# Batch 0's first steps reordered, one table set for exponential and logarithm, raw weights without a ring, later low parts beside main 0

## What is computed

```
x = x + ssm(layernorm(x))        # projection, depthwise conv + silu, selective scan over 512 rows, output product
x = x + ffn(layernorm(x))        # 8 experts: silu(x w_gate) * (x w_up), w_down, weighted by two softmaxes
x = x + attention(layernorm(x))  # 16 heads of 8, chunks of 10 rows, 25 rows to the left
x = x + ffn(layernorm(x))        # the same experts again
```

## Time and profile before

| | |
|---|---|
| median of 3 runs | 1492.82 us (1489.45 to 1494.48) |
| the profiled execution | 1493.85 us, span 1492.1 us |
| mean granted TensorE clock | 0.994 |
| PE busy | 1427.2 us, 96% |
| DVE, ACT, POOL busy | 950.3, 773.0, 504.3 us |
| first expert matmul (main 0) | 55.24 us |
| first expert matmul of main 1 | 143.2 us |
| table loads | 1.28 us each |

### The profile page before, as it was taken

The page is one execution under the profiler, slowest core; times in us unless marked ns, Lnnn a source line. Parts: engine busy times, 40 slices in busy tenths (PEclk is TensorE's granted clock), DMA queues, the critical chain, the costliest instruction groups (busy, mean ns, idle before and its releaser), DMA issues.

```text
span 1492.1 us, 31350 instructions
## 1 busy us (share of the span) xinstructions
PE 1427.2 (96%) x12756; PEld 1236.2 (83%) x12756; DVE 950.3 (64%) x2125; ACT 773.0 (52%) x1037; POOL 504.3 (34%) x446
## 2 busy tenths in 40 slices
PE   5798999999999999999999999999999999999998
PEld 3587878888788888888888888888888888888887
DVE  5655686665856667567675785658755565566543
ACT  6364738653466545645456574555644444355321
POOL 4351553433423443135410671136503320331000
PEclk9999999999999999999999999999999999999999
DMA  5120341004210420124002500062004200510000
GB/s 170 52 58 15 102 123 31 16 15 121 40 38 23 135 40 1 45 99 83 9 2 81 137 8 9 2 164 61 1 2 121 40 2 1 138 24 2 1 7 8
DMA packets 82876, 75.50 MB, mean 51 GB/s; under 512 B 5532, under 2 KB 60860, under 8 KB 82732
## 3 DMA queue, kind: packets, MB, share of 16 engines
q1 hardware_dynamic: 82732, 73.50, 18.8%
HBM read 60.65 MB, written 12.83 MB: 49 GB/s over the span
## 4 chain that ended last, share of the span: by engine, by line
PE 77%; DVE 10%; ACT 5%; issue 5%; POOL 4%; DMA 1%; DVEq 0%; SPq 0%; POOLq 0%; ACTq 0%
PE pd L1003 25%; PE pg L275 7%; PE pu L275 7%; PE pg L277 6%; PE pu L276 6%; PE pg L276 6%; PE pu L277 6%; PE att_ps L680 3%; DVE h L1096 2%; PE att_ps L702 2%; POOL arena L631 1%; PE att_ps L707 1%; DVE ffn_rows L298 1%; POOL arena L633 1%; DVE x L1084 1%
## 5 line engine op out<-in xcount | busy, mean ns | idle before, releaser
L1058 ACT ACTIVATE h<-pg 128x512 f32<-128x512 f32 x512 | 303.5, 597 | 658.3 <-PE pg L277 655.2
L1003 PEld LDWEIGHTS pd<-w_down,h 128*128 128x128 f32 x4096 | 512.2, 192 | 31.8 <-issue 2.7
L1003 PE MATMUL pd<-w_down,h 128*128 128x128 f32 x4096 | 525.0, 276 | 0.8 <-DVE x L1084 0.8
L1096 DVE TENSOR_TENSOR h<-h,pu 128x512 f32<-128x512 f32 x512 | 345.5, 679 | 215.4 <-PE pu L277 213.9
L275 PE MATMUL pg<-ffn_x_hi,w_gate_hi 128*128 128x512 f32 x512 | 244.5, 477 | 1.5 <-DVE ffn_x_lo L358 1.5
L275 PE MATMUL pu<-ffn_x_hi,w_up_hi 128*128 128x512 f32 x512 | 205.3, 401 | 13.4 <-DVE h L1096 13.2
L276 PE MATMUL pu<-ffn_x_lo,w_up_hi 128*128 128x512 f32 x512 | 203.3, 397 | 0.0
L276 PE MATMUL pg<-ffn_x_lo,w_gate_hi 128*128 128x512 f32 x512 | 203.3, 397 | 0.0
L277 PE MATMUL pg<-ffn_x_hi,w_gate_lo 128*128 128x512 f32 x512 | 203.0, 397 | 0.0
L277 PE MATMUL pu<-ffn_x_hi,w_up_lo 128*128 128x512 f32 x512 | 202.9, 396 | 0.0
L905 POOL TENSOR_TENSOR att_arena<-att_arena 128x512 f32<-128x512 f32 (+1 forms) x72 | 72.8, 1011 | 352.6 <-DVE att_arena L777 352.3
(11 more groups left out here) (192 smaller groups left out, 1540.2 us busy)
## 6 DMA issues: line engine op xcount, KB each, us to landing
arena<-bc_spread SPq DMA_DIRECT2D x56, 256.0 KB, 4.8
att_arena<-v_rows SPq DMA_DIRECT2D x64, 144.0 KB, 4.0
qk_rows<-qk_parts SPq DMA_DIRECT2D x32, 256.0 KB, 2.3
q<-qk_rows SPq DMA_DIRECT2D x32, 256.0 KB, 3.6
k<-qk_rows SPq DMA_DIRECT2D x32, 256.0 KB, 4.5
att_arena<-v_rows SPq DMA_DIRECT2D x64, 128.0 KB, 3.4
arena<-in_x SPq DMA_DIRECT2D x8, 256.0 KB, 2.9
x<-in_x SPq DMA_DIRECT2D x8, 256.0 KB, 3.4
```

The costliest lines, as they stand in the source:

```text
L1003: last = nc.tensor.matmul(pd[:, t * P:(t + 1) * P], h_b[:, d % NH, t * P:(t + 1) * P], wd[:, d % NCH, :], start=d % CPE == 0 and t == 0, s ...
L1058: nc.scalar.activation(h_b[:, c % NH, :], pg[c % 2][:, :], ACT.Silu).then_inc(gate_done, 1)
L1096: nc.vector.tensor_tensor(h, h, pu[d % 2][:, :], ALU.mult).then_inc(h_done, 1)
```

## The change

- The transposes of batch 0 come before the two products of small weights on PE, which are a job of their own now (slots -32.5 and -30.5); DVE's work on the second moves behind the convolution, and `w_small` counts one more step.
- PE makes the B/C product of batch 0 before the dt product.
- The SiLU of z moves behind the masked copy, for all batches, with a semaphore of its own (`silu_z`). The lower 64 rows of `zb` are set to zero once by POOL, and the z product reads all 128 rows.
- Behind tanh ACT loads the table set `natural_log_exp_and_others` explicitly; the copy of the tanh rows then comes before the exponential.
- The raw blocks have 16 places: the eight of `h_b` and eight in the part of the attention's buffer that is not in use yet. SP waits for none of them. Blocks alternate gate and up, so block j belongs to expert j // 2.
- ACT makes the high parts one slot earlier (from -33, ahead of the copy at -32.5).
- POOL makes the low parts 0 to 7 as before and the low parts 8 to 15 in slots -2 to 1, two in each. PE waits at every fourth chunk of main 0 for the two low parts of that expert; ACT waits at chunk 0 for eight.
- PE waits for `w_down` at the first down product.

The core of the diff:

```diff
+        w_raw = [h_b[:, i, :] for i in range(NH)] + [att_ar[:, N_S + i * L:N_S + (i + 1) * L] for i in range(2 * E - NH)]
...
                 if i == 0:
                     pe.wait_ge(w_small, 1)
+
+                    pe.wait_ge(xs_done, 1)
+                    for v in range(2):
+                        last = nc.tensor.matmul(pd[0:2 * DSTATE, :], wbc[v][:, :], xs, start=v == 0, stop=v == 1)
+                    last.then_inc(bc_raw, 1)
...
+                if i == 0:
+                    pe.wait_ge(pads_set, 9)
+                pe.wait_ge(silu_z, i + 1)
+
                 for t in range(TT):
-                    nc.tensor.matmul(ps[:, t * P:(t + 1) * P], zb[0:INNER, t * P:(t + 1) * P],
-                                     pk("w_out_z")[0:INNER, :], start=t == 0, stop=False)
+                    nc.tensor.matmul(ps[:, t * P:(t + 1) * P], zb[:, t * P:(t + 1) * P], pk("w_out_z"), start=t == 0, stop=False)
...
-                nc.scalar.activation(zb[0:INNER, :], cv[INNER:P, :], ACT.Silu).then_inc(silu_x, 1)
-                act.wait_ge(silu_x, 3 * i + 2)
+                act.wait_ge(silu_x, 2 * i + 2)
                 nc.scalar.activation(xsm, xb2, ACT.Copy, scale=pk("lo_ssm")).then_inc(xs_m, 1)
+                nc.scalar.activation(zb[0:INNER, :], cv[INNER:P, :], ACT.Silu).then_inc(silu_z, 1)
...
-                    rates(link)
+                    act.preload_act_table_set("natural_log_exp_and_others")
                     act.wait_ge(bc_set, 1)
                     nc.scalar.copy(bc_part[0], bc_t[:, :]).then_inc(bc_hi, 1)
+                    rates(link)
                     link.wait()
                     nc.scalar.activation(delta, delta, ACT.Ln, bias=1.0).then_inc(dt_soft, 1)
                     act.wait_ge(delta_done, 1)
+                    act.wait_ge(w_small, 2)
...
         def w_part(j, v):
-            return (wg, wu)[j // E][v][:, CPE * (j % E):CPE * (j % E + 1), :].rearrange("p a b -> p (a b)")
+
+            return (wg, wu)[j % 2][v][:, CPE * (j // 2):CPE * (j // 2 + 1), :].rearrange("p a b -> p (a b)")
...
                     if c == 0:
-                        pe.wait_ge(w_lo, 2 * E)
-                        pe.wait_ge(wd_loaded, 16 * E)
                         pe.wait_ge(pads_set, 8)
+                    if c < NCH and c % CPE == 0:
+                        pe.wait_ge(w_lo, 2 * (c // CPE + 1))
...
+                def small_weights(pe, link, k):
+
+                    yield T_SSM[0]["ln"] + 0.5
+                    pe.wait_ge(raw_packed, 16)
+                    nc.tensor.matmul(pg[0][:, 0:P], pk("w_dtx")[0:DTRANK, :], pk("w_dt")[0:DTRANK, :],
+                                     start=True, stop=True).then_inc(wdt_full, 1)
+                    yield T_SSM[0]["win"] + 0.5
...
-                        if j >= NH:
-                            sp.wait_ge(w_lo, j - NH + 1)
-                        sp.dma_start(h_b[:, j % NH, :], (wg_d, wu_d)[j // E][j % E]).then_inc(w_loaded[j % NH], 16)
+                        sp.dma_start(w_raw[j], (wg_d, wu_d)[j % 2][j // 2]).then_inc(w_loaded[j], 16)
...
                     if c < 0:
-                        if 0 <= c + SETUP - 8 < 2 * E:
-                            split_w(c + SETUP - 8)
+                        if 0 <= c + SETUP - 7 < 2 * E:
+                            split_w(c + SETUP - 7)
                         return
...
                 def chunk(c):
-                    if c < 0:
-                        j = c + SETUP - 8
-                        if 0 <= j < 2 * E:
+                    if c < 0 and 0 <= c + SETUP - 8 < NH:
+                        split_w(c + SETUP - 8)
+
+                    if -2 <= c < 2:
+                        for j in range(NH + 2 * (c + 2), NH + 2 * (c + 3)):
                             split_w(j)
-                        return
                     yield
...
+                pool.wait_ge(pads_set, 8)
+                nc.gpsimd.memset(zb[INNER:P, :], 0.0).then_inc(pads_set, 1)
+                pool.wait_ge(pads_set, 9)
```

More of the change, by code:

```diff
@@ L190, in build @@
         res_loaded = [sem(f"res_loaded{i}") for i in range(NXB)]
-        w_loaded, wd_loaded = [sem(f"w_loaded{i}") for i in range(NH)], sem("wd_loaded")
+        w_loaded, wd_loaded = [sem(f"w_loaded{i}") for i in range(2 * E)], sem("wd_loaded")
         w_hi, w_lo, w_small, w_prep, wdt_full = sem("w_hi"), sem("w_lo"), sem("w_small"), sem("w_prep"), sem("wdt_full")
@@ L203, in build @@
         bc_out = sem("bc_out")
-        silu_x, xs_m, xs_done = sem("silu_x"), sem("xs_m"), sem("xs_done")
+        silu_x, silu_z, xs_m, xs_done = sem("silu_x"), sem("silu_z"), sem("xs_m"), sem("xs_done")
         dt_soft, delta_done = sem("dt_soft"), sem("delta_done")
@@ L403, in pe @@
                 if i == 0:
-                    for v in range(2):
-                        last = nc.tensor.matmul(pd[0:2 * DSTATE, :], wbc[v][:, :], xs, start=v == 0, stop=v == 1)
-                    last.then_inc(bc_raw, 1)
                     yield at["k"][0] - 0.5
@@ L877, in pool @@
                 if j == 0:
-                    pool.wait_ge(w_small, 2)
+                    pool.wait_ge(w_small, 3)
                 heads = pk("head").unsqueeze(1).unsqueeze(3).broadcast_to([P, 4, 4, QW])
@@ L998, in chunk @@
                         pe.wait_ge(h_done, d + 1)
+                        if d == 0:
+                            pe.wait_ge(wd_loaded, 16 * E)
                         if d % CPE == 0 and d:
@@ L1008, in _ @@
                 pe.wait_ge(packed, 16)
[L1009 to L1015, removed]
+                def small_weights(pe, link, k):
[4 more added lines that the diff above has]
+                    yield T_SSM[0]["win"] + 0.5
+                    nc.tensor.matmul(pg[1][:, 0:P], pk("b_v").broadcast_to([P, P]), pk("w_o"),
+                                     start=True, stop=True).then_inc(bias_full, 1)
+                interleave([(small_weights, 0)] + [(Ssm.pe, i) for i in range(B)] + [(Att.pe, j) for j in range(B)] + [(Head.pe, m) for m in range(NM)], pe, None, chunk)
             @block.sync
@@ L1042, in split_w @@
                 def split_w(j):
-                    act.wait_ge(w_loaded[j % NH], 16 * (j // NH + 1))
-                    nc.scalar.copy(w_part(j, 0), h_b[:, j % NH, :]).then_inc(w_hi, 1)
+                    act.wait_ge(w_loaded[j], 16)
+                    nc.scalar.copy(w_part(j, 0), w_raw[j]).then_inc(w_hi, 1)
                 def chunk(c):
                     if c < 0:
-                        if 0 <= c + SETUP - 8 < 2 * E:
-                            split_w(c + SETUP - 8)
+                        if 0 <= c + SETUP - 7 < 2 * E:
+                            split_w(c + SETUP - 7)
                         return
@@ L1053, in chunk @@
                         if c == 0:
-                            act.wait_ge(w_lo, 2 * E)
-                            act.wait_ge(w_small, 2)
+                            act.wait_ge(w_lo, NH)
+                            act.wait_ge(w_small, 3)
                         if c >= NH:
@@ L1119, in small_weights @@
                     link(nc.vector.tensor_copy(u_b[:, 0, 0:P], pg[0][:, 0:P]))
-                    both([w[:, :] for w in wdt], u_b[:, 0, 0:P])
+                    link(nc.vector.tensor_copy(wdt[0][:, :], u_b[:, 0, 0:P]))
+                    nc.vector.tensor_tensor(wdt[1][:, :], u_b[:, 0, 0:P], wdt[0][:, :].bitcast(F32),
+                                            ALU.subtract).then_inc(w_small, 1)
+                    yield T_SSM[0]["win"] + 1.5
                     dve.wait_ge(bias_full, 1)
@@ L1125, in small_weights @@
                     nc.vector.tensor_scalar(neg_a[:, :], neg_a[:, :], -1.0, -1e-4, ALU.mult, ALU.add).then_inc(w_small, 1)
-                    dve.wait_ge(w_small, 1)
                     yield T_SSM[0]["y"]
@@ L1141, in split_w @@
                     pool.wait_ge(w_hi, j + 1)
-                    nc.gpsimd.tensor_tensor(w_part(j, 1), h_b[:, j % NH, :], w_part(j, 0).bitcast(F32),
+                    nc.gpsimd.tensor_tensor(w_part(j, 1), w_raw[j], w_part(j, 0).bitcast(F32),
                                             ALU.subtract).then_inc(w_lo, 1)
                 def chunk(c):
-                    if c < 0:
-                        j = c + SETUP - 8
-                        if 0 <= j < 2 * E:
+                    if c < 0 and 0 <= c + SETUP - 8 < NH:
+                        split_w(c + SETUP - 8)
+                    if -2 <= c < 2:
+                        for j in range(NH + 2 * (c + 2), NH + 2 * (c + 3)):
                             split_w(j)
-                        return
                     yield
```

## The result

| | before | changed |
|---|---|---|
| median | 1492.31 us (14 runs, 1488.67 to 1494.86) | 1485.82 us (14 runs, 1483.20 to 1489.76) |
| ratio to before | | 0.9954, 95% interval 0.9944 to 0.9965 |
| profiled execution | 1493.85 us, span 1492.1 | 1483.2 us, span 1481.4 |
| residual add of batch 0 | 48.62 us | 38.17 us |
| first expert matmul | 55.24 us | 48.62 us |

The change makes the kernel 6.5 us faster, 0.46%. The measured time lies inside the forecast's range of 1483.8 to 1494.8, but the forecast was 2.65 us faster, and it gave "within 0.3%" the largest chance. Both collisions of DVE's rows with POOL's low parts happened as forecast; what was too low is the rest of the gain.

A forecast was written before the change was run, and what follows sets the result against it. The prediction took a latency chain of batch 0 as the bound before 55.24 us, then PE. Its terms, -4.35 + 1.2 + 1.0 - 0.3 - 0.2 = -2.65 us from the median 1492.82, gave 1490.0 us, range 1483.8 to 1494.8.

The forecast's parts named there:

- within 0.3%: The outcome that the changed kernel differs from the one before by at most about 4.5 us; chance 0.55.
- Both collisions: DVE's rows in main 0's and batch 1's norms wait for POOL's low parts: 3.85 us more, then PE stands 1.2.
- Front: Start of batch 0: ACT's copy of the transposed rows starts at 9.6 to 9.65, gain 0.3 us, bounds 0 and 1.2.
- SiLU, order of the small products, tanh: Batch 0's chain: moving z's SiLU saves 0.6 us, B/C before dt 0.87; tanh comes about 1.6 us earlier.
- Tables: Between tanh and decays: one table set saves two loads of 1.28 us each; decays start at 23.5, 3.7 earlier.
- DVE without POOL: From batch 0's decays to residual add: with POOL silent, scans and products save 4.5 us; residual add at 40.4.
- a later rise of the clock: In main 0: PE's short stop puts off the rise to the high clock, costing 1.0 us, bounds 0 and 3.4.
- Rival C: Around main 0: held rows and PE's stops make the clock's rise fail, so the kernel is slower, 1497.5 us; chance 0.08.
- The z product: In the output product: reading 128 rows in place of 64, with as many matmuls and columns, costs nothing.
- the likeliest case: Both collisions happen and one table set serves between tanh and decays; 1487 to 1493 us, chance 0.50.
- rival A: Norms of main 0 and batch 1: no collision of DVE's rows with POOL's low parts; 1484.2 us, chance 0.25.

The follow-up runs named there:

- e5_z128_alone: The kernel before with one part alone: POOL zeroes the lower 64 rows of zb and PE's z product reads all 128; 1492.72 us, ratio 0.9994.
- e8_before_guard: The kernel before plus one wait: POOL waits for the four row blocks after its power in state space and expert norms; 1482.28 us, ratio 0.9927.
- e7_old_order: The changed kernel with z's SiLU again ahead of the masked copy and batch 0's dt product ahead of its B/C product; 1487.71 us, ratio 0.9973.
- e3_no_set: The changed kernel without the explicit load of the table set, so three loads stand between tanh and decays; 1488.15 us, ratio 0.9972.
- e2_low_early: The changed kernel with all 16 low parts made by POOL before main 0, directly behind the high parts; 1488.84 us, ratio 0.9973.
- e1_low_late: The changed kernel with low parts 8 to 15 made in slots 2 to 5, after a wait for batch 1's normalised rows; 1481.35 us, ratio 0.9929.
- e4_z64: The changed kernel with the z product read from 64 rows again, the zero fill kept; 1491.70 us, ratio 0.9990.

## Why the prediction was right and wrong, point by point

**Front.** Forecast: copy at 9.6, bound by a weight landing 6.3 us after its issue. Measured 8.62: the load landed after 5.3, and the cast and the transposes both ended at 8.6. Over all eleven profiles, with this or the old front, the copy starts anywhere from 8.4 to 9.95; the profile of before, from which I took the landing, was the latest. In e5_z128_alone and e8_before_guard, with the old front, it started at 9.09 and 8.66 and the first expert matmul came at 54.4 and 54.0, not 55.24. So about 1 us of the 6.6 us between the two profiles is the landings of two executions. One profile gave me one draw of a duration, and I used it as the value. Between the two profiles the term is 1.33, just outside its bounds of 0 and 1.2. Over the profiles the mean start is 8.75 with the new front (eight) and 9.23 with the old one (three), 0.5 apart, near the 0.3 of the forecast.

**SiLU, order of the small products, tanh.** Forecast 4.26 us from SiLU to tanh, measured 4.28; e7_old_order shows the 1.3 us of the two edits.

**Tables.** Forecast 4.32 from tanh to decays, measured 4.29; e3_no_set gives 2.2 for the two loads. The draining time that "ScalarE: Activation LUTs" of the Trainium skill adds to each load, in "What ACT_TABLE_LOAD costs", did not show: in e3_no_set the next operation starts within 0.02 us, three times.

**DVE without POOL.** Forecast 16.9 from decays to residual add, measured 15.8. The scans are 1.22 and the products 0.69 as forecast:

```profile
28.85 0.69 DVE L546 SCALAR_TENSOR_TENSOR arena<-x,arena 128x512 f32<-128x512 f32 x1
29.45 1.22 DVE L556 TENSOR_TENSOR_SCAN arena<-arena 128x512 f32<-128x512 f32 x1
```

I had left out one clip and one cast that were also slow beside POOL in the kernel before:

```profile
33.81 0.85 DVE L531 TENSOR_SCALAR x<-x 128x512 f32<-128x512 f32 x1
...
46.37 0.50 DVE L1104 CAST w_q_hi<-staged 128x128 fp32r<-128x128 f32 x1
```

In the changed kernel they take 0.42 and 0.22: 0.7 us. The last two blocks of the output product ran at the high clock (1.06 and 1.16 us for eight records, against 2.09), which kept PE out of the way; this is the 0.3 that the forecast had booked under the clock. e2_low_early puts the whole of it at 5.7 instead of 4.5.

**The collisions.** Forecast 5.0 us for the rows, measured 4.95; the last row of batch 1 forecast 1.2 us too late for PE, measured 1.5 (chunk 2 starts 7.88 us after chunk 0 instead of 6.39). e1_low_late takes both away. This step was right in mechanism and place, and in size for main 0's rows. What batch 1's rows cost by the end of main 0 is less sure. With them quick main 0 lasted 87.2 us in e2_low_early, where the clock rose 6.0 us after its start, and 88.2 in e1_low_late, where it rose after 8.2; with them slow it lasted 88.3, with the rise after 6.4. That is 0.1 to 1.1 us, against 1.2 forecast.

**What the stop does in main 0.** For the profiled execution the prediction was wrong here. I charged 1.0 us for a later rise of the clock. It rose 6.4 us after the first matmul, sooner than the 7.2 of before, and the 1.5 us were down to 0.7 by chunk 16 and 0.3 at the end of main 0; the cheaper z block and the earlier input of the small product are in that too. Rival C did not happen in it. But the late rise exists. e3_no_set and e4_z64 have the same two collisions, and in their profiles the clock rose 11.4 and 12.2 us after the first matmul and main 0 lasted 89.9 and 90.8 us. The changed kernel and e7_old_order, with the same collisions, rose after 6.4 and 6.3; the seven profiles without slow rows around main 0 lie between 6.0 and 8.9. In how many of the changed kernel's 14 runs the rise was late one profile can't tell, so the 1.0 is neither confirmed nor refuted for the median. (In rival C's sum, 14 us more at half speed make 1497.0, not 1497.5, and the border of +0.3% is 1497.3.)

**The z product.** Costed at nothing, with the reason that the number of matmuls and columns stays. That reason is false: e4_z64 shows 0.4 us per output product, e5_z128_alone 1.9 us in all. It is the one step whose mechanism I did not see, though the block of 64 rows was in the trace with its longer spacing. Why a block of 64 rows costs more was not tested.

**Sum.** The forecast's gain was 2.65. Add 1.9 for z and 0.8 for DVE's stretch (1.1 less the 0.3 that was booked under the clock). Add 1.4 for main 0: the forecast took 2.0 for it, the profiles show 0.3, and 0.3 of the difference is z's. That gives 6.8, against a measured 6.5. The agreement proves little, since two of the terms are read from single executions and the measured gain is one of medians.

That the range held is in part luck. 1485.8 lies below the 1487 to 1493 of the likeliest case; the range reached so far down for the sake of rival A (1484.2). Rival A was nearer in time than the likeliest case, but for a reason that is not its own: the rows did collide.

The clock's share of the measured difference can't be settled. The changed kernel ran 1485.8 to 1486.4 at a mean clock of 0.990 and 1483.2 to 1483.7 at 0.992 and 0.993, which is about 1484.8 at 0.991 (an estimate, halfway), where the one before ran 1488.4 to 1489.3. That is about 4 us at equal clock. A part of the 6.5 is that the changed kernel has runs at 0.992 and 0.993.

## What to carry to other kernels

When work moves from one engine's stretch to another, look at what the other engine has there in short dependent pieces: eight low parts cost DVE over 5 us beside scans, four of them nearly 4 beside main 0's rows, and they cost the rows nothing once POOL waits for these. A wait that lets the short critical operations go first can be worth more than the change it protects: one wait took 11 us off the kernel before. It pays only where the engine that bounds the kernel waits for those operations. One profile is one draw, of landings and of the clock: read a duration from several before it is used as a value. And a number of matmuls is not their cost: look at the spacing of starts around a block of another shape before it is called free.

## What the runs showed of the hardware

- DVE's row operations (fp32, 128 by 128, SBUF to SBUF) and POOL's operations take turns: with POOL's queue full each row ended 0.1 us after the POOL operation beside it. Four rows cost 4.95 us with low parts of 1.25 us, 1.11 with POOL waiting. POOL itself was not slowed by the rows (1.25 to 1.28 each).
- A block of four fp32 products with 64 contraction rows between products with 128 costs more than one with 128: 2.41 against 2.02 us for the stretch around it.
- The first load of 256 KB, issued at 2.7 us in each of the eleven profiles, landed 4.9 to 6.4 us later.
- The clock rose during the output product, at 32.4 to 35.5 us, in ten of the eleven profiles, those with the old start and with 64 rows among them, and fell again before main 0; only the profile of before shows no rise there. Stretches at 0.50, but for the one at the very end, last 3.4 or 6.8 us in the mains and 10.2 to 23.9 us around the start of main 0.
- The time of a run follows its mean granted clock in steps: the changed kernel took 1483.2 to 1483.7 us at 0.992 and 0.993, 1485.8 to 1486.4 at 0.990, 1487.6 to 1489.4 at 0.988, 1489.8 at 0.986. The mean can mislead: the profile of before, which has no rise ahead of main 0 and prints 1.00 until 62.4 though its matmuls run at the low level there, shows 0.994, and the runs of that kernel at 0.994 take 1493 to 1494.5. Most likely those, too, had no rise there.
